# Seams between the layers of a four-layer kernel: weights fetched one layer ahead, weight rounding inside the experts' stage, second batch prepared beside the first maxima

## The reference

```
layer 0: attn = multi-query attention (16 heads of 8) then Mamba (256 channels, 16 states); ffn = 32 experts of width 512, each
         fed by the gated sum over a batch's tokens (top 8 gates)
layer 1: attn = 16 heads of 64, causal; ffn = silu(xq @ wg.T) * (xq @ wu.T), rounded again, @ wd.T, where
         every operand (weights too: 352x128, 352x128, 128x352) is rounded blockwise to a 4-bit grid
layer 2: attn = 16 heads of 8, causal; ffn = top-1 routing to 8 experts with a capacity of 256 tokens
layer 3: attn = state-space scan, layernorm, projection; ffn = top-2 of 8 experts and 2 shared ones
```

## Time and profile before

| | us |
|---|---|
| median of 3 runs | 3028.58 (3024.81 to 3029.01) |
| the profiled execution | 3028.86 |
| its span in the profile | 3027.5 |
| start of layer 0 up to `mxT` of batch 0 | 22.3 to 73.2 |
| experts' stage | 1096.5 to 1162.3 |
| weights of layer 1 | 1162.4 to 1191.1 |
| start of layer 2 up to `mxT` of batch 0 | 2020.3 to 2081.6 |

### The profile page before, as it was taken

One profiled execution on the slowest core, in us unless ns is written; L12 is line 12 of the kernel. 1 busy time (PEld: TensorE's weight loads), 2 busy tenths in 40 slices (PEclk: granted clock), 3 DMA queues, 4 the chain that ended last, 5 costly groups with the idle time before them and its releaser, 6 DMA issues. The chain is left out here.

```text
span 3027.5 us, 47754 instructions
## 1 busy us (share of the span) xinstructions
PE 2419.8 (80%) x18201; PEld 1712.4 (57%) x18201; DVE 2214.6 (73%) x4587; ACT 1437.6 (47%) x3688; POOL 868.9 (29%) x453
## 2 busy tenths in 40 slices
PE   4788888888888675798888989867999986766766
PEld 2456555555566464466666666644666654544544
DVE  3488888888887844578787777754666634999998
ACT  0344545444544511466666676632334434555453
POOL 0033344434344420123232232310000001454543
PEclk9989999999999887799999999987999998888888
DMA  1011011101110154000000000000000002444443
GB/s 61 15 36 36 29 43 36 36 29 36 37 43 29 50 165 151 1 1 2 1 1 1 1 1 1 1 34 14 28 28 14 7 19 92 145 163 139 164 154 109
DMA packets 71348, 147.97 MB, mean 49 GB/s; under 512 B 6864, under 2 KB 37072, under 8 KB 70608
## 3 DMA queue, kind: packets, MB, share of 16 engines
q1 hardware_dynamic: 69072, 140.73, 13.8%
q0 software_dynamic: 2048, 4.20, 0.4%
HBM read 135.20 MB, written 9.18 MB: 48 GB/s over the span
## 5 line engine op out<-in xcount | busy, mean ns | idle before, releaser
L2091 POOL TENSOR_TENSOR h<-h,Crep 128x1024 f32<-128x1024 f32 x128 | 383.3, 3005 | 705.7 <-DVE h L1514 705.7
L2073 POOL TENSOR_TENSOR pr<-pr,rsum 128x512 f32<-128x512 f32 x192 | 227.5, 1188 | 617.6 <-DVE rsum L1358 617.6
L1392 DVE TENSOR_REDUCE mx<-psum 128x4 f32<-128x1024 f32 (+1 forms) x192 | 229.0, 1217 | 116.4 <-PE psum L656 116.4
L1514 DVE TENSOR_TENSOR_SCAN h<-dA,h 128x1024 f32<-128x1024 f32 x128 | 291.9, 2295 | 2.4 <-ACT dA L1977 1.8
L831 PE MATMUL psum<-h,pack_wf 128*128 128x256 f32 x1024 | 257.5, 409 | 5.4 <-POOL h L2091 5.4
L2125 POOL TENSOR_TENSOR h<-h,Crep 128x1024 f32<-128x1024 f32 x64 | 184.8, 2888 | 253.9 <-DVE h L1268 253.9
L831 PEld LDWEIGHTS psum<-h,pack_wf 128*128 128x128 f32 x1024 | 209.2, 209 | 43.0 <-POOL h L2091 6.4
L1880 ACT ACTIVATE pt<-psum 128x1024 f32<-128x1024 f32 x192 | 187.5, 1022 | 96.7 <-PE psum L658 96.7
L1836 ACT ACTIVATE pr<-psum,nb 128x256 f32<-128x256 f32 (+1 forms) x512 | 210.8, 429 | 46.5 <-DVE nb L1350 43.7
L1977 ACT ACTIVATE dA<-delta,A 128x255 f32<-128x255 f32 x512 | 210.2, 495 | 12.2 <-DVE h L1514 10.8
L1505 DVE TENSOR_TENSOR h<-dtu,psum 128x512 f32<-128x512 f32 x256 | 164.2, 676 | 69.1 <-PE psum L818 61.5
(11 more groups left out here) (342 smaller groups left out, 5446.1 us busy)
## 6 DMA issues: line engine op xcount, KB each, us to landing
Crep<-c_rows SPq DMA_DIRECT2D x64, 512.0 KB, 3.8
Brep<-bc_rows SPq DMA_DIRECT2D x64, 512.0 KB, 6.5
Crep<-bc_rows SPq DMA_DIRECT2D x64, 512.0 KB, 7.0
w1r<-m_w SPq DMA_DIRECT2D x32, 256.0 KB, 5.8
w2r<-m_w SPq DMA_DIRECT2D x32, 256.0 KB, 5.6
pack_wf<-wf SPq DMA_DIRECT2D x1, 3192.0 KB, 13.3
slots<-zero SPq DMA_DIRECT2D x12, 256.0 KB, 3.0
w1s<-s_w SPq DMA_DIRECT2D x8, 256.0 KB, 2.7
```

The source lines that it names most:

```text
L1392: ve.e.tensor_reduce(mx[:, qb, 2 * h:2 * h + 2, groups[0]:groups[-1] + 1], k.psum[:, base:base + 2, :].rearrange("p i (n x) -> p i n x", n ...
L1514: ve.e.tensor_tensor_scan(flat(h), flat(k.dA[c][g % 2]), flat(h), 0.0, ALU.mult, ALU.add).then_inc(*k.set("scanned", 0, b, g, c))
L2073: po.e.tensor_tensor(p3, p3, bcast(k.rsum[n][:, 0:len(heads[r])], P * (q + 1), 2), ALU.mult).then_inc(*k.set("normed", 1, b, p, r))
L2091: po.e.tensor_tensor(h[:, :, :], h[:, :, :], k.Crep[n % 3][:, :, :], ALU.mult).then_inc(*k.set("hC", 0, b, g, c))
```

## The change

- `layer0` and `layer2`: after batch 0's preparation, the steps of `first_max` (now with yields between score groups) are merged with batch 1's preparation on PE and DVE, in the orders `FIRST`. ACT keeps its order.
- `layer0`: at the end of its queue SP waits for batch 15's attention projection and issues `wf0e` and the loads of experts 0 to 7, whose buffers are placed over the attention's tiles; they no longer stand behind the barrier. In `experts0` SP now issues `wf1` first, then the loads of experts 8 to 31.
- The rounding of layer 1's weights moves into the experts' loop. Iterations 12, 17 and 22 start one rounding each (ACT's absolute value behind that iteration's gelu), and DVE runs up to three of its steps at the end of each iteration. Iterations 18, 19, 20, 23, 24, 25, 28, 29, 30 turn one of the nine pieces each on PE, copied by DVE at the end of the same iteration.
- `wf2` is issued by SP at the start of `layer1`, ahead of the zeroing of the routed rows.
- The memsets of `v` in layer 2 move from DVE to POOL, and DVE waits for them (`v_ones`) before it writes batch 0's `v`.

```diff
...
+FIRST = {
+    0: {"pe_pre0": (0, 2, 3, 4, 5, 7, 8, 9), "pe_first": (0, 1, 6, 10, 11),
+        "ve_pre0": (0, 1, 2, 3, 6, 7, 8, 9, 10, 11, 12, 13, 16, 17, 18), "ve_first": (0, 4, 5, 14, 15, 19, 20)},
+    2: {"pe_pre2": (0, 2, 3, 4, 5, 7, 8, 9, 11), "pe_first": (0, 1, 6, 10, 12),
+        "ve_pre2": (0, 1, 2, 3, 6, 7, 8, 9, 10, 11, 12, 13, 14, 15, 18, 19, 20) + tuple(range(23, 36)),
+        "ve_first": (0, 4, 5, 16, 17, 21, 22)},
+}
...
 LOADS = {"x": 0, "wf": 1, "wb": 2, "wf0": 3, "wfc": 0, "wf0e": 0, "wf1": 1, "wf2": 2, "wf3": 3}
...
     for c in range(3):
+        yield
         pe_quad(k, l, "max", 0, c)
+    yield
     pe_max_turn(k, l, 0)
...
     k.pre_read = ("x_mamba", b)
...
+QUANT_AT = (12, 17, 22)
+TURN_AT = (18, 19, 20, 23, 24, 25, 28, 29, 30)
...
 def pe_experts0(k):
...
             i.then_inc(*k.set("output0", e))
+        if ex in TURN_AT:
+            pe_weight1(k, TURN_AT.index(ex))
...
 def pe_ffn(k, b):
...
-def pe_weights1(k):
+def pe_weight1(k, i):
...
     pe, w, B6 = k.pe, k.w, k.bank[6]
...
+    pe.wait_ge(*k.at("fp4", "wd" if i >= 6 else "wgu", i % 6 // 3))
+    if i:
+        pe.wait_ge(*k.at("wT", i - 1))
+    rows = min(P, I1 - (i % 3) * P)
+    if i < 6:
+        x = pe.e.transpose(B6[:, 0:rows], k.wgu_q[0:rows, i, :], w["ident"][0:rows, 0:rows])
+    else:
+        x = pe.e.transpose(B6[0:rows, 0:P], k.wd_q[:, (i - 6) * P:(i - 6) * P + rows], w["ident"])
+    x.then_inc(*k.set("w_turned", i))
...
 def rows_in(ex):
...
     ve.wait_ge(*k.at("v_mm", 2, b, 1))
+    if b == 0:
+        ve.wait_ge(*k.at("v_ones"))
     if b >= 3:
...
     ve.e.tensor_tensor(k.v[b % 3][:, :, :, 0:8], bk[:, 0:L].rearrange("p (q h d) -> p q h d", q=QT, d=8),
...
         for h in range(2):
+            yield
             ve_max(k, l, 0, c, h)
...
             ve.e.tensor_tensor(k.oall[:, :, e], k.bank[2 + e % 2][:, 0:NB], bcast(w["m_b2"][:, e], NB, 1), ALU.add).then_inc(*k.set("oall", e))
+        if ex in QUANT_AT:
+            ve.wait_ge(*k.at(*landed("wf1")))
+            quant = ve_quant1(k, QUANT_AT.index(ex))
+            next(quant)
+        if ex >= QUANT_AT[0]:
+            for _ in range(3):
+                next(quant, None)
+        if ex in TURN_AT:
+            ve_weight1(k, TURN_AT.index(ex))
...
 def ve_fp4(k, name, b, out, src, nblk):
...
-def ve_weights1(k):
-    ve, w, B6 = k.ve, k.w, k.bank[6]
...
+def ve_quant1(k, i):
...
+    w = k.w
+    if i < 2:
+        return ve_fp4(k, "wgu", i, blocks(k.wgu_q[:, 3 * i:3 * i + 3, :]), blocks(w["wgu1"][:, 3 * i:3 * i + 3, :]), 3 * D // BLK)
+    return ve_fp4(k, "wd", 0, k.wd_q[:, :].rearrange("p (n k) -> p n k", k=BLK), w["wd1"].rearrange("p (n k) -> p n k", k=BLK), NBH)
...
+def ve_weight1(k, i):
+    ve, B6 = k.ve, k.bank[6]
+    rows = min(P, I1 - (i % 3) * P)
+    ve.wait_ge(*k.at("w_turned", i))
+    if i < 6:
+        x = ve.e.tensor_copy((k.wgT if i < 3 else k.wuT)[:, (i % 3) * P:(i % 3) * P + rows], B6[:, 0:rows])
+    else:
+        x = ve.e.tensor_copy(k.wdT[0:rows, i - 6, :], B6[0:rows, 0:P])
+    x.then_inc(*k.set("wT", i))
...
 def ve_ffn(k, b):
...
         ac.e.activation(k.hg[ex % 2][:, 0:H0 // P, :], k.hz[ex % 2][:, :, :], ACT.Gelu).then_inc(*k.set("hg", ex))
+        if ex in QUANT_AT:
+            ac_weights1(k, QUANT_AT.index(ex))
...
-def ac_weights1(k):
+def ac_weights1(k, i):
     ac, w = k.ac, k.w
     ac.wait_ge(*k.at(*landed("wf1")))
-    ac_abs(k, "wgu", 0, blocks(w["wgu1"][:, 0:3, :]), 3 * D // BLK)
-    ac.wait_ge(*k.at("fp4", "wgu", 0))
-    ac_abs(k, "wgu", 1, blocks(w["wgu1"][:, 3:6, :]), 3 * D // BLK)
-    ac.wait_ge(*k.at("fp4", "wgu", 1))
-    ac_abs(k, "wd", 0, w["wd1"].rearrange("p (n k) -> p n k", k=BLK), NBH)
+    if i:
+        ac.wait_ge(*k.at("fp4", "wgu", i - 1))
+    if i < 2:
+        ac_abs(k, "wgu", i, blocks(w["wgu1"][:, 3 * i:3 * i + 3, :]), 3 * D // BLK)
+    else:
+        ac_abs(k, "wd", 0, w["wd1"].rearrange("p (n k) -> p n k", k=BLK), NBH)
...
 def ac_ffn(k, b):
...
-def sp_experts0(k):
+def sp_experts0(k, some):
     sp = k.sp
-    for ex in range(E0):
+    for ex in some:
         s = ex % 8
...
             sp.wait_ge(*k.at("hidden0", ex - 8))
...
-def layer0(k):
+def layer0(k, t0e):
     k.slot_read, k.pre_read = [None] * 4, None
-    for pre in (pe_pre0, ve_pre0, ac_pre0):
+    for e, pre, first in (("pe", pe_pre0, pe_first_max), ("ve", ve_pre0, ve_first_max)):
         run(pre(k, 0))
-        run(pre(k, 1))
-    pe_first_max(k, 0)
-    ve_first_max(k, 0)
+        merge(FIRST[0], (first(k, 0), e + "_first"), (pre(k, 1), e + "_pre0"))
+    run(ac_pre0(k, 0))
+    run(ac_pre0(k, 1))
     ac_max_taken(k, 0, 0)
...
         turn0(k, t, "pe", pe_pre0, pe_out, pe_wide0, pe_inner, pe_states, pe_results, pe_summing)
...
     sp_layer0(k)
+    k.sp.wait_ge(*k.at("proj", 0, NB - 1))
+    sp_load(k, "wf0e", t0e)
+    sp_experts0(k, range(8))
     for q in (k.pe, k.ve, k.ac, k.po, k.sp):
...
-def experts0(k, t0e, t1):
-    sp_load(k, "wf0e", t0e)
-    sp_experts0(k)
+def experts0(k, t1):
     sp_load(k, "wf1", t1)
+    sp_experts0(k, range(8, E0))
     k.ac.e.preload_act_table_set("gelu_and_others")
...
     ve_experts0(k)
...
-def layer1(k):
+def layer1(k, t2):
     k.ac.e.preload_act_table_set("natural_log_exp_and_others")
-    k.pe.wait_ge(*k.at(*landed("wf1")))
+    sp_load(k, "wf2", t2)
     k.po.e.memset(k.zero[:, :], 0.0).then_inc(*k.set("zeroed"))
     sp_zero_rows(k)
-    pe_weights1(k)
-    ve_weights1(k)
-    ac_weights1(k)
     for pre, spread in ((pe_pre1, pe_spread1), (ve_pre1, ve_spread1), (ac_pre1, ac_spread1)):
...
         run(spread(k, 1))
...
-def layer2(k, t2, t3):
-    sp_load(k, "wf2", t2)
+def layer2(k, t3):
     sp_load(k, "wf3", t3)
     for v in k.v:
-        k.ve.e.memset(v[:, :, :, 9:], 0.0)
-        k.ve.e.memset(v[:, :, :, 8:9], 1.0)
+        k.po.e.memset(v[:, :, :, 9:], 0.0)
+        i = k.po.e.memset(v[:, :, :, 8:9], 1.0)
+    i.then_inc(*k.set("v_ones"))
     k.ve.e.memset(k.run[:, 0, :], 0.0)
...
     k.slot_read, k.pre_read = [None] * 4, None
-    for pre in (pe_pre2, ve_pre2, ac_pre2):
+    for e, pre, first in (("pe", pe_pre2, pe_first_max), ("ve", ve_pre2, ve_first_max)):
         run(pre(k, 0))
-        run(pre(k, 1))
+        merge(FIRST[2], (first(k, 2), e + "_first"), (pre(k, 1), e + "_pre2"))
+    run(ac_pre2(k, 0))
+    run(ac_pre2(k, 1))
+    ac_max_taken(k, 2, 0)
     po_scatter(k, 0)
     po_scatter(k, 1)
-    pe_first_max(k, 2)
-    ve_first_max(k, 2)
-    ac_max_taken(k, 2, 0)
     for t in range(NB + 1):
...
         turn2(k, t, "ve", ve_pre2, ve_wide, ve_out)
...
     load(k, packs)
-    layer0(k)
...
     t1 = k.pack("wf1")
...
     k.hz, k.hg = k.two("hz", [P, H0 // P, NB]), k.two("hg", [P, H0 // P + P // NB - 1, NB])
-    experts0(k, t0e, t1)
+    layer0(k, t0e)
...
     place_ffn(k)
-    layer1(k)
+    experts0(k, t1)
...
+    t2_at = (k.top + 4095) // 4096 * 4096 + 8192
+    k.top = t2_at
+    t2 = k.pack("wf2")
+    layer1(k, t2)
...
     inner = k.top
-    t2 = k.pack("wf2")
     place_common(k, 2)
     place_route(k)
-    layer2(k, t2, t3)
+    assert k.top <= t2_at
+    layer2(k, t3)
...
     place_common(k, 3)
```

More of the change, by code:

```diff
@@ L933, in pe_ffn @@
     i.then_inc(*k.set("down1", b))
-def pe_weights1(k):
+def pe_weight1(k, i):
     pe, w, B6 = k.pe, k.w, k.bank[6]
-    for i in range(9):
-        pe.wait_ge(*k.at("fp4", "wd" if i >= 6 else "wgu", i % 6 // 3))
-        if i:
-            pe.wait_ge(*k.at("wT", i - 1))
-        rows = min(P, I1 - (i % 3) * P)
-        if i < 6:
-            x = pe.e.transpose(B6[:, 0:rows], k.wgu_q[0:rows, i, :], w["ident"][0:rows, 0:rows])
-        else:
-            x = pe.e.transpose(B6[0:rows, 0:P], k.wd_q[:, (i - 6) * P:(i - 6) * P + rows], w["ident"])
-        x.then_inc(*k.set("w_turned", i))
+    pe.wait_ge(*k.at("fp4", "wd" if i >= 6 else "wgu", i % 6 // 3))
[7 more added lines that the diff above has]
+    x.then_inc(*k.set("w_turned", i))
 def rows_in(ex):
@@ L1619, in blocks @@
     return ap.rearrange("p q (n k) -> p (q n) k", k=BLK)
-def ve_weights1(k):
-    ve, w, B6 = k.ve, k.w, k.bank[6]
-    ve.wait_ge(*k.at(*landed("wf1")))
-    for i in (0, 1):
-        run(ve_fp4(k, "wgu", i, blocks(k.wgu_q[:, 3 * i:3 * i + 3, :]), blocks(w["wgu1"][:, 3 * i:3 * i + 3, :]), 3 * D // BLK))
-    run(ve_fp4(k, "wd", 0, k.wd_q[:, :].rearrange("p (n k) -> p n k", k=BLK), w["wd1"].rearrange("p (n k) -> p n k", k=BLK), NBH))
-    for i in range(9):
-        rows = min(P, I1 - (i % 3) * P)
-        ve.wait_ge(*k.at("w_turned", i))
-        if i < 6:
-            x = ve.e.tensor_copy((k.wgT if i < 3 else k.wuT)[:, (i % 3) * P:(i % 3) * P + rows], B6[:, 0:rows])
-        else:
-            x = ve.e.tensor_copy(k.wdT[0:rows, i - 6, :], B6[0:rows, 0:P])
-        x.then_inc(*k.set("wT", i))
+def ve_quant1(k, i):
[12 more added lines that the diff above has]
+    x.then_inc(*k.set("wT", i))
 def ve_ffn(k, b):
```

## The result

The changed kernel takes 2976.22 us (median of 4 runs, 2970.13 to 2981.11) against 3028.26 for the kernel before (median of 4, 3024.81 to 3029.01). The ratio is 0.9828, with a 95% interval of 0.9816 to 0.984; the prediction said 2979.4, 2969 to 2991. The profiled execution took 2981.11 with a span of 2979.8, so the two profiled executions are 47.75 us apart (forecast 49.2) and lie at the upper end of their runs. The medians are 52.0 us apart.

A forecast was written before the change was run, and what follows sets the result against it. It took single steps waiting for one another at the seams beside the barriers as the bound. Terms -8.0 - 7.9 + 5.6 - 28.6 - 5.1 - 5.2 = -49.2 us from median 3028.58 gave 2979.4, range 2969 to 2991.

The forecast's parts named there:

- Start of layer 0: Layer 0's merged order of batch 1's preparation and first score groups: `mxT` earlier, 8.0 us off, bounds 5 and 10.
- Layer 0 to the experts: Prefetched expert weights: PE starts 3.1 us earlier and stays at the fast clock, 4.8 more; 7.9 off, bounds 3.1 and 8.
- `wf1` ahead of expert 8: Weight queue in the experts' stage: expert 8's weights still come in time; cost 0, bounds 0 and 4.4 us.
- Rounding: Layer 1's weight rounding inside the experts' loop: 5.2 + 1.7 + 0.8 - 2.1, costs 5.6 us, bounds 3.5 and 9.
- No reload of ACT's table: ACT's absolute value in the experts' loop needs no table load; otherwise six loads of 1.28 us, none in the sum.
- Start of layer 1: First spreading matmul starts with layer 1's barrier, no longer after the rounding: 28.6 us off, bounds 27.5 and 30.
- Seam to layer 2: Layer 2's statistics start at once, with `wf2` early and memsets on POOL: 5.1 us off, bounds 4.7 and 5.2.
- Merged start of layer 2: Layer 2's merged order, from statistics to `mxT`: 5.2 us off, bounds 3 and 8.
- (a): Rival: clock rises in both merged starts, first spreading steps run fast, experts' loop reaches 3.5; about 2970 us, chance 0.13.
- (b): Rival: merged orders in layers 0 and 2 bring nothing, 13.2 us lost; 2992.5 us, chance 0.16 including a part of it.
- (c): Rival: experts' weights come late behind `wf1`, +4.4 us, 2984 us; counted within the forecast's 0.68.
- (d): Rival: DVE's roundings open gaps on PE, clock falls for iterations 12 to 31; slower than before, 3042 us, chance 0.02.

## Why the prediction was right, point by point

The mechanism held at every seam, save for how one term splits between clock and waiting, and no term had the wrong sign. Two sizes were off, both so that the change brings more than forecast: the rounding by 1.9 us, the merged start of layer 2 by 2.5 to 3.5.

- **Start of layer 0, -8.0.** Measured -8.0, and 8.6 on average over eleven traces. The walk put `mxT` at 66.1 at the slow rate and took 1.3 more for the clock. Among kernels with this start it comes at 60.8 to 65.1; against before's 72.8 two of the eight traces (60.8 and 62.1) pass the bound of 10, both where more of the matmuls ran fast.
- **Layer 0 to the experts, -7.9.** 8.0 by the kernel that rounds in layer 1. The sum was right and its reason half: 2.4 us of the 4.8 were clock. I counted all 9.3 us between 1099.89 and 1109.18 as slow matmuls, but 0.73 of them are a wait for the second expert's weights, which stands in before's trace, and slow matmuls covered 1.3 more of the same wait. The prefetch takes away both, so the sum came out right although its split was wrong.
- **`wf1` ahead of expert 8, 0.** Right: no matmul waits for a load in the changed kernel. It hangs on the prefetch; without it the same queue costs 5.15 us and a second fall of the clock.
- **Rounding, +5.6.** Measured 3.7, nearly the lower bound of 3.5. The step that failed is the one for the full-width iterations (5.2 - 2.1). I had three late outputs of about 1 us each; PE shows them late by 0.57, 0.31 and 0.28, for `hz` and `hg` are double and DVE works off its backlog. The transposes cost 0.11 each and not 0.26, with some waits for copies added. The sign that I gave, iterations 13 to 15 some 2.3 us long, did not come: they kept 1.79, and the delay fell on 16 (1.87) and 17 (2.46), when DVE had fallen far enough behind.
- **No reload of ACT's table.** The Trainium skill ("ScalarE: Activation LUTs", "Table sets: the hidden batching unit") has abs in every table set. The trace agrees: between the loads at 1089.14 and 1150.68 there is none, at the absolute value of 1111.38 or elsewhere.
- **Start of layer 1, -28.6.** Measured -28.6. The chain behind it was to stay the same and was 0.7 us shorter.
- **Seam to layer 2, -5.1.** Measured -5.3, and +5.4 when undone. POOL's memsets take 0.71 and `xn` beside them 0.62, against 0.60 with no memset beside it (above). The Trainium skill ("SBUF — State Buffer", "Who interferes with whom") has the pair of ports block a whole instruction only where both engines use it; a statistic with one input is outside, `xn` might have been inside. In the row of 1985.84 `xn` runs beside the memset that starts at 1985.61; it takes 0.02 longer, and no wait of a memset's length shows.
- **Merged start of layer 2, -5.2.** Measured -7.7 and 8.7 on average, the worst miss of size together with the rounding. The step that was mis-sized is the clock: the walk named it ("some 3 more") and I left it out, and it rose in all eight merged traces, each of which is shorter than the 50.6 that 55.8 - 5.2 gives. The part that I counted against the order was there: the idle matmuls at 2029.39 take 2.72 us on the path.
- **What I said would make me wrong** was a change in the length of layer 0's or layer 3's turns, or PE at its slow rate inside the experts. None of these came: +0.6 from `mxT` to the last X update of layer 0, +1.0 behind layer 2's `mxT`, 1.00 in the experts' stage. But the sign was weak: two traces of the same program differ by 3.6 us in that piece of layer 0 (1023.7 and 1027.4). And it did not name layer 1, which moved by 5.3. Its turns stayed, 48.55 us per batch in both kernels; only the ends of the layer moved.
- **The rivals.** (a), a clock up nearly everywhere, came true in part: in layer 2's start, and in the experts' loop, which it put at 3.5 (3.7 measured). (b) fell, by 8.6 us at each start. (c), weights late behind `wf1`, fell: no matmul of the experts waits for a load. (d) fell, the clock reads 1.00 through the experts' stage.

## What to carry to other kernels

Behind a barrier, read the first steps for what they wait for and for PE's clock together: a slow clock can cover late data, so keeping the clock up alone brought 2.4 us where the prefetch, which ended both, brought 8.0. Work moved into a loop whose engine has room can cost little: work that had kept DVE busy for 22.2 us cost 3.7 in pieces of three steps and 2.0 in pieces of two, of which 1.0 is what PE's own transposes take; but its data has to be there, and the transfer that brings it must not stand ahead of the loop's own. And where a start has only single dependent steps on PE, filling its pauses with idle matmuls pays: at the three starts together it was worth 27 to 29 us, about as much as moving the rounding (28.6 less 3.7).
